# Relu features of the second layer dealt out anew over VectorE, GpSimd and ScalarE

## The reference, cut to what matters

```python
q = jnp.einsum('bnc,ac->bna', X, Wq)
k = jnp.einsum('bnc,ac->bna', X, Wk)
e = jax.nn.relu(_rho_signed_sqrt(q[:, :, None, :] + k[:, None, :, :]))
scores = jnp.einsum('bija,a->bij', e, Wphi)
ex = jnp.exp(scores - m)
denom = jnp.sum(ex, axis=-1)
part1 = jnp.einsum('bij,bjc->bic', ex, Vy)
Ew = jnp.einsum('bij,bija->bia', ex, e)
part2 = jnp.einsum('bia,ca->bic', Ew, We_w) + We_b * denom[..., None]
```

## Time and profile before

| | |
|---|---|
| median of 3 runs | 1483.0 us (1482.01 to 1483.51) |
| profiled execution, its time | 1496.05 us |
| profiled execution, span on the core | 1494.3 us |
| busy: PE, DVE, ACT, POOL | 82%, 86%, 78%, 53% |
| TensorE's granted clock, mean | 0.959 |

### The profile page before, as it was taken

The page is one execution under the profiler, slowest core; times in us unless marked ns, Lnnn a source line. Parts: engine busy times, 40 slices in busy tenths (PEclk is TensorE's granted clock), DMA queues, the critical chain, the costliest instruction groups (busy, mean ns, idle before and its releaser), DMA issues.

```text
span 1494.3 us, 25209 instructions
## 1 busy us (share of the span) xinstructions
PE 1229.9 (82%) x6185; PEld 575.0 (38%) x6185; DVE 1280.2 (86%) x3505; ACT 1158.9 (78%) x1324; POOL 789.9 (53%) x1166
## 2 busy tenths in 40 slices
PE   2798687878864788899888988899888998899887
PEld 1476455555541233333333333333333333333333
DVE  5686687878866689999999999999999999999997
ACT  1566576767725689998899899998899998998960
POOL 2702100000000278878788777888788877887730
PEclk7899899999977799999999999999999999999998
DMA  5002200000000000000000000000000000000001
GB/s 183 13 1 34 16 1 0 0 0 0 0 1 18 7 19 26 19 18 21 26 23 18 18 28 25 18 18 18 28 25 18 18 28 25 18 18 18 28 25 32
DMA packets 38780, 31.58 MB, mean 21 GB/s; under 512 B 6150, under 2 KB 35609, under 8 KB 38738
## 3 DMA queue, kind: packets, MB, share of 16 engines
q1 hardware_dynamic: 37714, 29.76, 6.7%
q0 software_dynamic: 1024, 1.35, 1.0%
HBM read 29.10 MB, written 2.75 MB: 21 GB/s over the span
## 4 chain that ended last, share of the span: by engine, by line
DVE 30%; PE 26%; issue 9%; DVEq 3%; ACT 1%; POOL 0%; ACTq 0%
DVE arena L1024 17%; PE ps L1304 9%; PE ps L1317 7%; DVE arena L1010 6%; PE ps L1361 4%; PE ps L1381 2%; PE ps L1353 2%; DVE x L1067 2%; PE ps L1335 2%; DVE z L1050 2%; DVE spread L1076 1%; DVE nmax L1016 1%; DVEq L1023 1%; DVEq L1067 1%; ACT arena L1161 1%
## 5 line engine op out<-in xcount | busy, mean ns | idle before, releaser
L1024 DVE SCALAR_TENSOR_TENSOR arena<-arena,ps 128x512 f32<-128x512 f32 x1024 | 663.1, 679 | 65.9 <-PE ps L1317 65.7
L1161 ACT ACTIVATE arena<-arena,eps 128x4096 f32<-128x4096 f32 x128 | 474.3, 3709 | 38.6 <-POOL arena L1284 38.1
L1317 PE MATMUL ps<-spread,sel 128*128 128x512 f16 x1024 | 348.5, 386 | 118.4 <-DVE arena L1024 112.1
L1278 POOL TENSOR_SCALAR arena<-kT,negq 128x512 f32<-128x512 f32 x480 | 331.6, 701 | 196.5 <-DVE arena L1024 181.3
L1284 POOL TENSOR_SCALAR arena<-arena,q 128x512 f32<-128x512 f32 x480 | 351.8, 743 | 22.4
L1304 PE MATMUL ps<-arena,phi_cols 128*32 128x512 f32 x2048 | 276.4, 614 | 20.2 <-ACT arena L1161 20.2
L1317 PEld LDWEIGHTS ps<-spread,sel 128*128 128x128 f16 x1024 | 92.1, 97 | 513.0 <-DVE arena L1024 438.4
L1149 ACT ACTIVATE arena<-kT,q 128x512 f32 (+1 forms) x330 | 217.8, 715 | 3.0
L489 ACT ACTIVATE kT<-ps,region 128x512 f32<-128x512 f32 x128 | 88.2, 689 | 101.3 <-DVE region L559 97.7
L1270 POOL TENSOR_SCALAR negq<-q 128x256 f32<-128x256 f32 x4 | 3.5, 870 | 297.6 <-POOLq L762 297.6
L1010 DVE TENSOR_SCALAR arena<-kT,q 128x512 f32 (+1 forms) x214 | 141.9, 686 | 0.3 <-PEq L762 0.3
(11 more groups left out here) (196 smaller groups left out, 1794.9 us busy)
## 6 DMA issues: line engine op xcount, KB each, us to landing
wge<-in_e_wg SPq DMA_DIRECT2D x32, 256.0 KB, 2.7
w1e<-in_e_w SPq DMA_DIRECT2D x32, 128.0 KB, 2.1
w2e<-in_e_w SPq DMA_DIRECT2D x32, 128.0 KB, 2.1
w3e<-in_e_w SPq DMA_DIRECT2D x32, 128.0 KB, 2.1
region<-in_w SPq DMA_DIRECT2D x1, 2048.0 KB
out<-x SPq DMA_DIRECT2D x4, 256.0 KB, 2.7
region<-in_wqk SPq DMA_DIRECT2D x1, 512.0 KB, 4.6
region<-in_wv SPq DMA_DIRECT2D x1, 512.0 KB, 5.3
```

The costliest lines, as they stand in the source:

```text
L1024: dve.scalar_tensor_tensor(feat[:, j, k, :], feat[:, j, k, :], 1.0, psB[:, k % BANKS, :], ALU.mult, ALU.mult, accum_out=sums[:, j, gg, c:c ...
L1161: act.activation(grp, grp, ACT.Sqrt, bias=eps[:]).then_inc(e_ready, 2)
L1278: pool.tensor_scalar(feat[:, j, QUADS * gg + c, :], kT[:, b * N:(b + 1) * N], HUGE, negq[:, b % 2, at - b * N // 2:at - b * N // 2 + 1], A ...
L1317: pe.matmul(psB[:, k % BANKS, :], sel[:, gg, c, :], spread[:, j, :], start=True, stop=True).then_inc(bc_done, 1)
```

## The change

The two lists, and with them the third:

```diff
-    ON_POOL = [2, 2, 2, 2, 2, 2, 2, 2]
-    ON_DVE = [1, 0, 1, 1, 0, 1, 1, 0]
+    ON_POOL = [2, 3, 2, 2, 2, 3, 2, 2]
+    ON_DVE = [0, 0, 1, 0, 0, 0, 1, 0]
     ON_ACT = [QUADS - d - p for d, p in zip(ON_DVE, ON_POOL)]
```

## The result

The changed kernel takes 1490.09 us (4 runs, 1489.11 to 1490.24) against 1482.63 for the kernel before: ratio 1.0048, 95% interval 1.0031 to 1.0066, slower by 7.5 us. I had forecast 1497, slower by 14. The direction held and the size came out at half, but not by the forecast's way: the steady blocks are nearly as long as before, and most of the loss is something the forecast didn't have, TensorE's clock. Two of the terms of its sum were wrong too.

A forecast was written before the change was run, and what follows sets the result against it. TensorE and VectorE bound the kernel in turn, by waits around a circle. -0.86 + 1.32 = +0.46 us a block, times 30 = +13.8 us, on the 1483.0 median: 1496.8, taken as 1497; range 1477 to 1508.

The forecast's parts named there:

- The circle and its closing point: TensorE sets the pace from (0,0) to (3,0), VectorE from there to (7,2), where TensorE's broadcast for (0,0) waits.
- Feature at (4,0): Removed from VectorE's part, with TensorE's next broadcasts ready: -0.86 us a block.
- Group 5, +1.32: VectorE's feature at (6,0) gone, GpSimd's third added: the lift queued behind delays silu and (7,1), together +1.32 us a block.
- a wait of 1.76: VectorE's wait at (7,0) for GpSimd's lift, once a block, 1.76 us.
- The feature at (7,0): VectorE's feature waits for GpSimd's first cut of group 6 and lasts about 0.9 us in place of 0.47.
- Feature at (1,0): Removed where VectorE waits for TensorE: 0 us; the wait of 0.41 at (3,0) becomes 0.97.
- Feature at (3,0): Stays on VectorE, falls into GpSimd's second cut of group 2 and ends like today: 0, bounded by -0.22.
- Rival 1: VectorE's feature at (3,0) gets cheap: +0.24 us a block, 7 us, 1490; chance 0.17.
- the longer idle time before (0,0): TensorE's wait before (0,0) becomes about 2.0 us (1.55 + 0.46).
- Group 1, 0: Three features on GpSimd, one less on ScalarE: later root absorbed by waits, 0 with a margin.
- a sign against the forecast: The forecast is wrong if TensorE waits for ScalarE's roots, or no wait on line 1260 shows.

The follow-up runs named there:

- The two runs on this point: Kernel before with group 0's feature moved from VectorE to ScalarE, 1477.17 us; kernel before with VectorE's first product at (1,1) instead of (1,2), 1485.69 us.
- group 5 alone: Kernel before with only group 5's feature moved from VectorE to GpSimd: 1555.1 us, ratio 1.0491.
- The four parts alone: Kernel before with one group's feature moved per run: group 0 1477.17 us, group 1 1465.69, group 3 1458.28, group 5 1555.1.
- that one digit: Changed kernel with LIFT_AT 5 instead of 6, GpSimd's two lifts ahead of its group 5 features: 1455.15 us, ratio 0.9811.
- a third: Kernel before with groups 0 and 1 changed, group 5 as before, group 3's feature moved from VectorE to GpSimd: 1487.34 us, ratio 1.0019.

## Why the prediction was right in part and its sum wrong

The forecast said slower because a block would grow by 0.46 us. A steady block grew by 0.05, which makes 1.5 us of the 7.5, inside what one measurement can tell. Most of the rest came from TensorE's clock, which the prediction doesn't have. So the sum was some 12 us too high by two gains that it put at 0 (0.18 and 0.21 us a block) and some 5 us too low by the clock. That the direction held is mostly luck.

**The circle and its closing point: right.** VectorE waits for the lift at (7,0) in every block, and it goes away with the order of GpSimd's queue alone. I forecast a wait of 1.76; it is 1.40, because TensorE's broadcast already holds VectorE 0.18 us at (7,0) and the rest of VectorE's lead was smaller too. That changes nothing for (7,1), since GpSimd's queue sets it.

**Feature at (4,0), -0.86: right** (-0.85 in the changed kernel, -0.86 alone).

**Group 5, +1.32: right**, 1.26 measured in both kernels that have it. The feature at (7,0) fell into the first cut of group 6 as worked out, and VectorE went on 0.21 us behind that cut (1109.55 + 0.68 = 1110.23, (7,1) at 1110.44). The Trainium skill ("SBUF — State Buffer", section "Who interferes with whom") would have the loser blocked for the whole instruction, which makes it 0.18 longer, as a feature costs 0.39 when free: with its 0.21 the row stands against that figure, though with the rule that the feature must wait.

**Feature at (1,0), "gone: 0": the first step that failed.** It measured -0.18. I took a stretch in which VectorE waits for TensorE at both ends as TensorE's alone. But TensorE waited inside it too, 0.42 us a block (11.0 in 26) at a weight load. The matmuls beside it show no idle time, so not all of it counts; 0.18 is what the block gains when the wait goes. Most of the rest of VectorE's 0.56 became a wait for TensorE, though not where I had put it: 0.29 at (2,3), nothing more at (3,0). The two runs on this point show that VectorE's work from (1,0) to (1,2) is on the path, by the product and by the reduction (1,2).

**Feature at (3,0), "0, bounded by -0.22": the second.** I had 0.04 us of margin between the two cases and took the wrong one, in part because of the first: TensorE reaches (3,0) 0.18 earlier, so the feature begins 0.55 after GpSimd's first cut of group 2 (1125.18 to 1125.73), where I had 0.71. It cost 0.43 less, of which TensorE's broadcast for (4,0) took back 0.22, as the bound had it. Rival 1 named this and its size, and its time of 1490 is the measured one; but that agreement is partly luck. With both failures the sum is -0.86 + 1.26 - 0.21 - 0.18 = +0.01 a block (0.05 measured), not the +0.24 of rival 1; the clock made up the difference.

**TensorE's clock: missing altogether, though it is most of the measured loss.** The sum put the clock at nothing: it counted the longer idle time before (0,0) at its own length. And it had that length wrong, 2.0 us for the 2.53 measured, because it added the growth of the whole block, 0.46, to the 1.55. What counts is the delay between (7,0) and (7,2), which TensorE spends idle: with group 5 alone it is 2.83 = 1.55 + 1.28. In the changed kernel it is 0.3 less, because there the scores ahead of it start 0.31 later, held by ScalarE's root. TensorE in the changed kernel, to hold against its rows at 1116 under "Group 5 alone":

```profile
1077.11 0.82 PE L1317 MATMUL ps<-spread,sel 128*128 128x512 f16 x3
1078.17 1.06 PE L1304 MATMUL ps<-arena,phi_cols 128*32 128x512 f32 x8 [0.24 <-ACT arena L1161]
```

In two blocks of 30 the clock fell around that idle time. 4.2 us in the trace, about 5 by the medians.

**Group 1, 0: not shown.** I had named as a sign against the forecast that TensorE waits for roots. It does, 0.73 us a block (19.1 in 26), but right ahead of its idle time before (0,0), where TensorE would stand idle next in any case. Alone the group is worth -17 us, through features that get cheap at (3,0) and (4,0). In the changed kernel the one at (4,0) is gone, so most of that can't come. The four parts alone sum to -0.23 - 0.54 - 0.83 + 1.26 = -0.34 us a block, all four together to about +0.05: they aren't additive. (The 1.26 leaves the clock out.)

## What to carry to other kernels

Work given to an engine with time to spare isn't free when something short stands behind it in that engine's queue and another engine waits for it: look at what the queue does next, not at the busy share. Put the short, awaited work first; here that one digit was worth 35 us. And when a wait grows on the engine that feeds TensorE, look at the granted clock in the stretch behind it before calling the rest unexplained.

## What the runs showed of the hardware that I had not expected

- TensorE's clock fell to 1.2 GHz around single idle times under 3 us: of 2.83 us in 19 of 28 blocks of one kernel, of 2.5 us in 2 of some 30 of another, of 2.4 to 2.6 us in 9 of some 30 of a third, and in the steady blocks never around the 1.55 us of the kernel before. In the first of these it fell 0.4 to 1.6 us behind the idle time, in the other two 0.2 to 0.9 us before its end. Each fall cost 1.3 to 2.8 us. Why it fell around some idle times and not around others of the same length stays open.
- Six useless matmuls a block in that idle time gave 39 us in one kernel, 10 in another, and 5 in the kernel before, whose steady blocks had no low clock.
- The same feature instruction of VectorE's costs from 0.39 to 0.86 us by where it begins in GpSimd's running instruction. Moving one feature from ScalarE to GpSimd, in another group, gave 17 us by that alone.
